# Two-layer mixture-of-experts kernel: reordering the last attention window, its chunks and its weight split

## The chip, the cores and the metric

One core of a Trainium2 chip runs the whole program. The metric is the device time of one execution in microseconds; the median of three runs of the kernel before is 1303.91 us (1302.14 to 1304.94).

## The reference, cut to what matters

`x` holds 2 sequences of 1024 tokens with 256 features. Six residual steps follow one another: half a mixture of experts (8 experts, top 2), an RWKV-like attention, half the same mixture; then for the second layer:

```python
x = x + 0.5 * _L1_ffn_ref(_layernorm(x), ...)    # 32 experts of width 96, top 6, and a shared expert of width 192
x = x + _L1_attn_ref(_layernorm(x), ...)
x = x + 0.5 * _L1_ffn_ref(_layernorm(x), ...)    # the same weights again
# _L1_attn_ref: Q, K, V = split(X @ W_in.T + b_in); Q, K = rope(Q), rope(K)
#   A = sum over tokens of (K / |K|) * V;  Y = A * Q;  return Y @ W_out.T + b_out + X
# _L1_ffn_ref: scores = sigmoid(x @ gate_w); top 6, weights normed to 1
#   routed = sum over the chosen experts of weight * (silu(x wg) * (x wu)) wd;  shared = silu(x sg) * (x su) @ sd
```

The attention needs a sum over all 1024 tokens of a sequence before any of its outputs.

## The kernel before, in words

The tokens lie in SBUF as `XT`, 16 tiles of 128 tokens; a block `b` is four tiles (512 tokens), and two blocks make a sequence. The four mixtures are f = 0 to 3. Each engine has its own instruction stream, written out by hand, and semaphores tie them; a stream is strictly in order, so an instruction that waits holds all that stand behind it on its engine.

A mixture f has two parts. In its preparation, for each block: the norm's statistics (`stats`, DVE, lines 1839 to 1849), root and reciprocal (`std`, ACT; `offsets`, DVE, 1854 and 1856), the normed rows `xnt` (`rows`, ACT, line 1360), their transposes (`turn`, PE, 757 to 762, eight transposes of 128x128, of which all wait for the fourth tile of rows), a copy and a high and low half (`plain`, `split_high` on ACT, 1749 and 1752; `split_low` on DVE, 2497), the gate logits (`logits_of`, PE), `score` (ACT), `chosen` (DVE, 1890 to 1931: the top 6 as a mask), `rank` (PE, sums over tokens), `slots` (DVE, 1933 to 2009: each token's place in the table of its expert, written by line 1986). Then POOL scatters the rows of `xnt` to DRAM (`scatter_tile`, line 638), one indirect DMA per tile and choice, 24 per block and 96 for f = 3. `slots(3, 3)` ends with eight short steps that find each pair's expert. The shared expert is worked off in chunks, two per block (`gate_up`, `down` on PE; `silu`, `hidden` on ACT; `prod`, `low_hidden`, `finish` on DVE, `finish` adding the sum to `XT` at line 2061).

In the second part, `tiles(f)`, SP loads pairs of 128 gathered tokens (line 545), PE turns them, computes gate and up (`up`, line 910) and down, and POOL gathers the results (line 653). For f = 3 the down weights are split in a high and a low part first: `down_high` (ACT, 1501, four copies), `down_back` (ACT, 1509, eight copies of the high part into PSUM), `down_low` (DVE, 2523, eight subtractions). The second `up` of `tiles(3)` and the first down wait for all eight.

Between `tiles(2)` and `tiles(3)` stands the window. It holds the attention and the whole preparation of mixture 3. For each block g PE makes eight sets in PSUM banks n % 4 (`attend`: k1, k2, v1, v2, ss, q1, q2, rn); DVE rotates k1 and q1 (`rotated`, 2454 to 2458), weights the values (`key_values`, `key_inverse`), and sums them against rn (`key_sums`, 2479). After both blocks of a sequence `weighted` makes `WSH` (2487), `project_out` multiplies it with the queries (PE, 1256) into banks 0 to 3, and `added` adds it to `XT` (2493), one call for two tiles. POOL adds the attention's own norm as a residual (`residual(b)`, 658 and 660, for blocks 2 and 3 in this window) once the rows of block b are there, and it stands ahead of the scatters in POOL's stream. The chunks of mixture 3 follow the routing, one at the logits of block 2 and the rest behind block 3's `chosen`, with the parts of the down split between them. SP waits for all scatters and for the last `finish` before it loads for `tiles(3)`.

Of the kernel before, what the change touches and what calls it, by code (L numbers as in the profile page):

```python
# [6 lines left out]
F32 = mybir.dt.float32  # L7
# [25 lines left out]
PARTS0 = 0  # L33
HALVED0 = 0
# [42 lines left out]
TAKEN = {"k1": 3, "v1": 4, "v2": 5, "q1": 8, "rn": 10}  # L77
# [14 lines left out]
def chunk_table():  # L92
# [35 lines left out]
def program(nc, x_in, w0s, w0e, wsq, wa0, w1, wsh1, win, wout, gate0, gate1, vecs, rope, bcol, brow, ident_in, tri_in, cvec_in, xd, yd, out):  # L128
# [21 lines left out]
    with ExitStack() as ctx:  # L150
# [127 lines left out]
        xh31_at = upto[0]  # L278
        XH[3, 1] = inside("XH3_1", [P, 2, KD, BT], F32R)
        assert upto[0] <= tb_end, (upto[0], tb_end)  # L280
# [12 lines left out]
        XH[3, 2] = inside("XH3_2", [P, 2, KD, BT], F32R)  # L293
        XH[3, 3] = inside("XH3_3", [P, 2, KD, BT], F32R)
        S3 = inside("S3", [P, 2, BT], F32)
        HL3 = inside("HL3", [P, 2, 2, BT], F32R)
        assert upto[0] <= xh31_at
# [13 lines left out]
        TX, TGU, THT, TY = 0, 1, 3, 7  # L311

# [193 lines left out]
        def _(sp):  # L506
# [86 lines left out]
            sp.wait_ge(CK.sum, GROUP["s", 3, 3] + 1)  # L593
# [160 lines left out]
        def _(pe):  # L754
            mm = nc.tensor.matmul

            def turn(norm, b, src, bank):
                pe.wait_ge(norm.rows, NT * (b + 1))
                for k in range(KD):
                    for a in range(NT):  # L760
                        last = nc.tensor.transpose(ps[:, bank + k, a * P:(a + 1) * P], src[:, b * NT + a, k * P:(k + 1) * P], ident[:, :])  # L761
                last.then_inc(norm.turned, 1)
# [101 lines left out]
            def tiles(f, beside=None, ahead=None, between=None):  # L864
# [16 lines left out]
                def hturned(q):  # L881
                    pe.wait_ge(TL.hid, q + 1)
                    pe.wait_ge(TL.hT, q)
                    if f == 3:
                        pe.wait_ge(TL.hlo, HALVED0 + q - q0)
# [7 lines left out]
                def up(q):  # L893
# [6 lines left out]
                    if f == 3 and i == 1:  # L900
                        pe.wait_ge(ew_lo, PARTS0 + 8)
# [12 lines left out]
                def down_rows(q):  # L914
# [3 lines left out]
                    if f == 3:  # L918
                        if q == q0:
                            pe.wait_ge(ew_lo, PARTS0 + 8)  # L920
                        pe.wait_ge(TL.hlo, HALVED0 + q - q0 + 1)
# [295 lines left out]
            def attend(s, n0, n1):  # L1217

                for n in range(n0, n1):
# [5 lines left out]
                    elif s:  # L1225
                        pe.wait_ge(A1.add, n + 1)
# [20 lines left out]
            def project_out(s):  # L1247
                pe.wait_ge(A1.wo, s + 1)
                pe.wait_ge(A1.qrot, 2 * s + 2)
                pe.wait_ge(A1.q2, 2 * s + 2)  # L1250
                for h in range(ST // 2):
                    for i in range(2):
                        a = ((2 * h + i) % NT) * P
                        dst = ps[:, h, i * D:(i + 1) * D]
# [31 lines left out]
            def window():  # L1286
                n = len(SETS)
                chunks = [ch for b in range(NB) for ch in RUN["s", 3, b][0]]
                attend(0, 0, 2 * n)
# [29 lines left out]
                gate_up(chunks[1], taken_over(chunks[1]))  # L1319
                down(chunks[0])  # L1320
                next_rank(3)
                for i in range(2, len(chunks)):
                    gate_up(chunks[i], taken_over(chunks[i]))
                    down(chunks[i - 1])
                    if i == 3:
# [23 lines left out]
        def _(act):  # L1349
# [147 lines left out]
            def down_high(g):  # L1497
                if g == 0:
                    act.wait_ge(CK.gu, RUN["s", 3, 0][0][-1].i + 1)
                    act.wait_ge(A1.add, 8)  # L1500
                fn(WDH[:, 8 * g:8 * g + 8, :], WDR[:, 8 * g:8 * g + 8, :], ACT.Copy).then_inc(ew_hi, 1)

            def down_back(g):
                act.wait_ge(ew_hi, g // 2 + 1)
                if g:
                    act.wait_ge(ew_lo, g)
# [251 lines left out]
            def window():  # L1758
# [30 lines left out]
                split_high(2)  # L1789
                score(3, 2, A_BANK + 1)  # L1790
                rows(F_NORM[3], 3, XT[:, tiles_of(3), :])
                plain(3)
                split_high(3)
                score(3, 3, A_BANK + 1)
                for i, ch in enumerate(chunks):
                    silu(ch)
                    hidden(ch)
                    if i % 2:
                        down_high(i // 2)
                    if i >= 3:  # L1800
                        down_back(i - 3)
                for g in (5, 6, 7):
                    down_back(g)
# [15 lines left out]
        def _(dve):  # L1819
# [654 lines left out]
            def key_sums(g):  # L2474
                A1.ready(dve, g, "rn")
                dve.wait_ge(A1.taken, TAKES * g + TAKEN["q1"])
# [4 lines left out]
                dve.wait_ge(A1.taken, TAKES * (g + 1))  # L2481
# [8 lines left out]
            def added(s, h):  # L2490
                rows = XT[:, s * ST + 2 * h:s * ST + 2 * h + 2, :].rearrange("p t d -> p (t d)")
                dve.wait_ge(A1.y, 4 * s + h + 1)
                tt(rows, rows, ps[:, h, :], ALU.add).then_inc(A1.add, 1)
# [23 lines left out]
            def down_low(g):  # L2517
                dve.wait_ge(ew_back, g + 1)
                if g == 0:
# [5 lines left out]
            def window(first):  # L2525
# [17 lines left out]
                key_inverse(0)  # L2543
                rotated(0, "q1", QT[:, 0, 0, :], A1.qrot)
                key_sums(0)
# [11 lines left out]
                added(0, 0)  # L2557
                added(0, 1)
                dve.wait_ge(A1.add, 2)
                stats(F_NORM[f], 0, XT[:, tiles_of(0), :])  # L2560
                added(0, 2)
                offsets(F_NORM[f], 0, True)
# [158 lines left out]
```

## Time and profile before

| what | value |
|---|---|
| median of three runs | 1303.91 us |
| profiled execution: span | 1495.7 us |
| PE busy, DVE, ACT, POOL | 1178.6, 743.8, 536.0, 596.8 us |
| mean granted PE clock | 0.865 |
| window between `tiles(2)` and `tiles(3)` | about 998 to 1262 us |

Times in a view of the trace are microseconds from the start of the span, durations in its groups nanoseconds. The profiled execution has no time of its own beside its span. PE and PEld are matmul and weight load, DVE VectorE, ACT ScalarE, POOL GpSimd, SP the queue that issues plain DMAs. `[x <- y]` behind an instruction is how long its engine stood idle before it and what ended that.

### The profile page before, as it was taken

How to read it: one execution, taken by the hardware profiler on the slowest of the kernel's cores; microseconds unless marked ns; L12 is line 12 of the kernel's file. 1: busy time of each engine (PE TensorE's matmuls, PEld its weight loads, DVE VectorE, ACT ScalarE, POOL GpSimd, SP SyncE). 2: the span in 40 equal slices, each digit the busy share in tenths (PEclk: the TensorE clock that was granted, in tenths of full speed). 3: DMA queues.
4: the chain of work that ended last, by engine and by line, in shares of the span. 5: the costliest groups of instructions: out<-in, count | busy, mean ns of one | idle time of the engine just before them, and what ended most of it. 6: DMA issues, size and time to landing. Idle time of an engine off the chain costs nothing.

```text
span 1495.7 us, 20198 instructions
## 1 busy us (share of the span) xinstructions
PE 1178.6 (79%) x6031; PEld 960.0 (64%) x6031; DVE 743.8 (50%) x2333; ACT 536.0 (36%) x1012; POOL 596.8 (40%) x579
## 2 busy tenths in 40 slices
PE   4799988979989898854768998897755436988884
PEld 4677755666778676633557987875434225978784
DVE  5553465564546536413445555678644214633443
ACT  2323344554533234321413433442303115644442
POOL 3661352211124213674550155662453730045554
PEclk9789999998989999865868999898875667998897
DMA  9523439400002573331426687760121212676676
GB/s 331 211 72 107 143 96 308 141 1 0 1 29 107 206 260 119 117 114 64 173 76 216 195 241 237 219 191 4 60 79 41 105 53 63 198 208 205 204 223 191
DMA packets 125302, 209.81 MB, mean 140 GB/s; under 512 B 15296, under 2 KB 104768, under 8 KB 123328
## 3 DMA queue, kind: packets, MB, share of 16 engines
q1 hardware_dynamic: 100624, 141.38, 28.7%
q0 software_dynamic: 24576, 67.14, 14.4%
q8 instruction: 56, 0.92, 0.3%
q14 instruction: 46, 0.38, 0.1%
HBM read 129.29 MB, written 101.19 MB: 154 GB/s over the span
## 4 chain that ended last, share of the span: by engine, by line
PE 48%; DVE 18%; issue 13%; another core or an unknown queue 10%; ACT 6%; POOL 3%; DMA 1%; SPq 0%; DVEq 0%; POOLq 0%; ACTq 0%
PE ps L910 15%; PE ps L932 6%; PE ps L877 5%; PE ps L817 4%; PE ps L829 4%; PE ps L889 3%; PE ps L1093 2%; PE ps L1100 2%; ACT xnt L1360 1%; PE ps L927 1%; PE ps L1244 1%; DVE HL L2047 1%; POOL xd L638 1%; PE ps L925 1%
## 5 line engine op out<-in xcount | busy, mean ns | idle before, releaser
L653 POOL DMA_INDIRECT G<-yd,slot_of x256 | 253.1, 989 | 424.6 <-issue 189.3
L638 POOL DMA_INDIRECT xd<-xnt,slot_of x256 | 251.4, 982 | 224.4 <-DVE slot_of L1986 136.9
L910 PE MATMUL ps<-WE,xT 128*128 x1016 | 200.7, 343 | 5.6 <-issue 3.9
L2102 DVE TENSOR_TENSOR hid<-hid,ps 128x192 f32<-128x192 f32 (+2 forms) x168 | 65.4, 389 | 247.9 <-ACT hid L1551 198.1
L910 PEld LDWEIGHTS ps<-WE,xT 128*128 128x128 f32 x1016 | 174.0, 202 | 9.9 <-issue 9.7
L1522 ACT ACTIVATE xT<-ps 128x512 f32<-128x512 f32 (+1 forms) x168 | 99.2, 590 | 156.9 <-PE ps L877 121.6
L877 PE MATMUL ps<-ident,xd_in 128*128 128x128 f32 x664 | 108.2, 287 | 44.2 <-ACT xT L1522 24.0
L2081 DVE SCALAR_TENSOR_TENSOR XT<-G,wt,XT 128x256 f32<-128x256 f32 x256 | 123.8, 494 | 27.5 <-DMA G<-yd,slot_of 17.0
L1551 ACT ACTIVATE hid<-ps 128x192 f32<-128x192 f32 (+2 forms) x168 | 60.4, 359 | 192.1 <-PE ps L910 139.9
L877 PEld LDWEIGHTS ps<-ident,xd_in 128*128 128x128 f32 x664 | 84.5, 148 | 60.6 <-issue 37.0
L1379 ACT ACTIVATE S<-ps 128x512 f32<-128x512 f32 (+1 forms) x72 | 42.6, 592 | 179.1 <-PE ps L817 140.1
L910 PE MATMUL ps<-W0E,xT 128*128 x312 | 103.3, 475 | 0.1
L2109 DVE COPY yo<-ps 128x512 f32<-128x512 f32 x104 | 70.9, 682 | 59.6 <-PE ps L932 30.7
L2047 DVE TENSOR_TENSOR HL<-S,HL 128x512 fp32r<-128x512 f32 (+1 forms) x72 | 51.9, 721 | 92.8 <-ACT HL L1388 87.0
L817 PE MATMUL ps<-XH,W0S 128*128 128x512 f32 x288 | 87.5, 456 | 8.9 <-issue 7.1
L932 PE MATMUL ps<-W0E,hT 88*128 x312 | 80.0, 401 | 13.3 <-issue 10.0
L889 PE MATMUL ps<-ident,hid 128*96 128x128 f32 (+1 forms) x410 | 75.5, 282 | 17.1 <-issue 7.6
L1388 ACT ACTIVATE HL<-S 128x512 fp32r<-128x512 f32 (+1 forms) x72 | 45.0, 625 | 104.8 <-DVE S L2042 70.7
L932 PEld LDWEIGHTS ps<-W0E,hT 88*128 88x128 f32 x312 | 61.6, 200 | 29.0 <-issue 15.1
L761 PE MATMUL ps<-ident,xnt 128*128 128x128 f32 x232 | 40.4, 332 | 50.3 <-ACT xnt L1360 41.3
L817 PEld LDWEIGHTS ps<-XH,W0S 128*128 128x128 f32 x288 | 62.7, 224 | 26.3 <-issue 12.0
L910 PEld LDWEIGHTS ps<-W0E,xT 128*128 128x128 f32 x312 | 58.7, 198 | 28.3 <-issue 5.1
(245 smaller groups left out, 2173.6 us busy)
## 6 DMA issues: line engine op xcount, KB each, us to landing
xd_in<-xd SPq DMA_DIRECT2D x164, 256.0 KB
yd<-yo SPq DMA_DIRECT2D x164, 256.0 KB
WE<-w SPq DMA_DIRECT2D x8, 1280.0 KB
W0E<-w0e SPq DMA_DIRECT2D x1, 4864.0 KB
xd<-xnt,slot_of POOLq DMA_INDIRECT x256
G<-yd,slot_of POOLq DMA_INDIRECT x256
W0E<-w0e SPq DMA_DIRECT2D x1, 3040.0 KB
XT<-x_in SPq DMA_DIRECT2D x4, 512.0 KB, 6.1
```

Of the source, the lines that this page charges most:

```text
L638: nc.gpsimd.indirect_dma_start(xd[f // 2][:, :], bass.IndirectOffsetOnAxis(ap=slot_of[:, t, k:k + 1], axis=0), xnt[:, t, :], None).then_in ...
L653: nc.gpsimd.indirect_dma_start(G[:, n % G_RING, :], None, yd[f // 2][0:min(ly.early[t][k] * 2, ly.TILES) * P, :], bass.IndirectOffsetOnAxi ...
L817: last = mm(ps[0:ch.H, ch.bank + u, :], l, r, start=(i == 0), stop=(i == len(terms) - 1))
L877: last = nc.tensor.transpose(ps[:, TX, (2 * a + k) * P:(2 * a + k + 1) * P], xd_in[:, q % X_RING, a, k * P:(k + 1) * P], ident[:, :])
L889: last = nc.tensor.transpose(ps[0:ly.part, hth, n * P:(n + 1) * P], hid[:, q % 2, a, c * ly.part:(c + 1) * ly.part], ident[:, :])
L910: last = mm(dst, xT[:, q % 2, a, k, :], flat[:, bass.ds(expert[2 * q + a] + k * 2 * ly.H, 2 * ly.H)], start=(k == 0), stop=(k == KD - 1))
L932: last = mm(ps[:, ty, a * D:(a + 1) * D], hT[0:ly.part, q % 2, a * ly.parts + c, :], flat[0:ly.part, bass.ds(expert[2 * q + a] + ly.down_a ...
L1522: fn(xT[:, q % 2, 0:m].rearrange("p a k t -> p (a k t)"), ps[:, TX, 0:m * D], ACT.Copy).then_inc(TL.xT, 1)
L2047: tt(hl[0:ch.H, 1, ch.i % 2, :], S_of[ch.kind][0:ch.H, ch.i % 2, :], hl[0:ch.H, 0, ch.i % 2, :].bitcast(F32), ALU.subtract).then_inc(CK.lo, 1)
L2081: stt(XT[:, t, :], G[:, n % G_RING, :], wt[:, t, k:k + 1], XT[:, t, :], ALU.mult, ALU.add).then_inc(g_used, 1)
L2102: tt(hid[:, q % 2, 0:m, 0:ly.H], hid[:, q % 2, 0:m, 0:ly.H], src, ALU.mult).then_inc(TL.hid, 1)
L2109: copy(yo[:, q % Y_RING, 0:m].rearrange("p a d -> p (a d)"), ps[:, down_bank(f, q), 0:m * D]).then_inc(TL.y, 1)
```

## The change

- `turn` waits for the rows tile by tile and transposes tile by tile; it is used in all four preparations and in both attentions.
- In the window `key_sums` comes before `rotated(g, "q1")` on DVE, and `rotated` of the second block behind `weighted`. Bank q1 is thus taken last and rn earlier.
- `project_out` waits for the queries of its half only and writes to banks 0, 4, 1, 2. `summed(b)` adds two tiles, takes their `bn_stats`, and again, for each half. Block 0's sums and `offsets` come before the statistics of the attention norm's block 3, whose root and rows move on ACT behind the rows of block 0 and `score(3, 0)`; POOL's `residual(3)` waits for them.
- Chunks 0, 1 and 2 stand between the routing steps of blocks 2 and 3 on PE, ACT and DVE. Chunks of blocks 0 and 1 use banks 2 and 3 alone. `down_high` stands behind chunks 4 to 7, `down_back` and `down_low` behind all chunks, in the order 2 to 7, 0, 1.
- SP waits for the last `gate_up` in place of the last `finish`. Some buffers move (`XH[3, 2]` to QT, `XH[3, 3]` to KB, `HL3` to the place of a staging buffer).

```diff
-            add(("s", f, b), ("s1", "s3")[f - 2], f, b, SH1, (2, 6))
+            add(("s", f, b), ("s1", "s3")[f - 2], f, b, SH1, (2, 6) if f == 2 or b >= 2 else (2, 2))
+        OUT_BANK = (0, A_BANK, 1, 2)
+        SPLIT_ORDER = (2, 3, 4, 5, 6, 7, 0, 1)
@@ sync
-            sp.wait_ge(CK.sum, GROUP["s", 3, 3] + 1)
+            sp.wait_ge(CK.gu, RUN["s", 3, 3][0][-1].i + 1)
@@ tensor
             def turn(norm, b, src, bank):
-                pe.wait_ge(norm.rows, NT * (b + 1))
-                for k in range(KD):
-                    for a in range(NT):
+                for a in range(NT):
+                    pe.wait_ge(norm.rows, NT * b + a + 1)
+                    for k in range(KD):
...
             def project_out(s):
                 pe.wait_ge(A1.wo, s + 1)
-                pe.wait_ge(A1.qrot, 2 * s + 2)
-                pe.wait_ge(A1.q2, 2 * s + 2)
                 for h in range(ST // 2):
+                    if h % 2 == 0:
+                        pe.wait_ge(A1.qrot, 2 * s + 1 + h // 2)
+                        pe.wait_ge(A1.q2, 2 * s + 1 + h // 2)
...
-                gate_up(chunks[0], taken_over(chunks[0]))
+                chunk(0)
                 logits_of(2)
                 next_turn(3)
                 next_rank(2)
+                chunk(1)
                 logits_of(3)
+                chunk(2)
+                next_rank(3)
                 pe.wait_ge(F_NORM[3].lo, NB)
...
-                for i in range(2, len(chunks)):
+                for k in range(3, len(chunks)):
@@ scalar
-                std(AT_NORM, 3)
-                rows(AT_NORM, 3, XT[:, tiles_of(3), :])
                 flipped(2, B_BANK)
                 std(F_NORM[3], 0)
                 rows(F_NORM[3], 0, XT[:, tiles_of(0), :])
+                std(AT_NORM, 3)
                 std(F_NORM[3], 1)
                 plain(0)
                 split_high(0)
                 score(3, 0, A_BANK + 1)
+                rows(AT_NORM, 3, XT[:, tiles_of(3), :])
                 rows(F_NORM[3], 1, XT[:, tiles_of(1), :])
...
+                for i in range(8):
+                    down_back(i)
@@ vector
+            def summed(b):
+                s = b // 2
+                for i in range(2):
+                    h = 2 * (b % 2) + i
+                    added(s, h)
+                    dve.wait_ge(A1.add, 4 * s + h + 1)
+                    for a in (2 * i, 2 * i + 1):
+                        last = nc.vector.bn_stats(st6[:, a, :], XT[:, b * NT + a, :])
...
-                rotated(1, "q1", QT[:, 1, 0, :], A1.qrot)
                 key_sums(1)
                 weighted()
+                rotated(1, "q1", QT[:, 1, 0, :], A1.qrot)
+                summed(0)
+                offsets(F_NORM[f], 0, True)
                 last_stats()
                 offsets(AT_NORM, 3, True)
...
+                summed(1)
                 offsets(F_NORM[f], 1, True)
...
                 chosen(f, 2)
+                prod(chunks[0])
+                low_hidden(chunks[0])
                 slots(f, 2, A_BANK)
                 split_low(3)
+                prod(chunks[1])
                 chosen(f, 3)
-                prod(chunks[0])
-                low_hidden(chunks[0])
+                low_hidden(chunks[1])
+                finish(chunks[1])
+                prod(chunks[2])
                 slots(f, 3, A_BANK)
+                low_hidden(chunks[2])
...
+                for i in range(8):
+                    down_low(i)
```

## Rows read from the trace of the kernel before

**Rows 1.** The profile's page: the span, and the chain of waits by engine.
```profile
span 1495.7 us, 20198 instructions
...
PE 48%; DVE 18%; issue 13%; another core or an unknown queue 10%; ACT 6%; POOL 3%; DMA 1%; SPq 0%; DVEq 0%; POOLq 0%; ACTq 0%
```
**Rows 2.** The chain of waits, 1061 to 1262 us: start, length, what.
```profile
1123.98 10.92 another core or an unknown queue
...
1185.53 32.93 another core or an unknown queue
```
**Rows 3.** Timeline of POOL: start us, us, engine, line, operation [idle before it <- releaser].
```profile
1061.77 1.01 POOL L638 DMA_INDIRECT xd<-xnt,slot_of  x1 [18.36 <-DVE slot_of L1986]
...
1101.22 0.96 POOL L638 DMA_INDIRECT xd<-xnt,slot_of  x1 [9.33 <-DVE slot_of L1986]
...
1153.94 0.96 POOL L638 DMA_INDIRECT xd<-xnt,slot_of  x1 [22.72 <-DVE slot_of L1986]
...
1213.44 0.96 POOL L638 DMA_INDIRECT xd<-xnt,slot_of  x1 [0.30 <-issue]
```
**Rows 4.** Timeline of DVE, third norm's routing: `chosen(3, 0)`, slots of blocks 0 and 3.
```profile
1052.03 0.20 DVE L1898 MAX8 t<-sc 128x8 f32<-128x40 f32 x1 [1.08 <-issue]
...
1061.31 0.18 DVE L1986 TENSOR_SCALAR slot_of<-v 128x32 int32<-128x32 f32 x1
...
1170.46 0.18 DVE L1986 TENSOR_SCALAR slot_of<-v 128x32 int32<-128x32 f32 x1
```
**Rows 5.** Timeline, end of the window and start of `tiles(3)`.
```profile
1218.49 1.22 DVE L2061 SCALAR_TENSOR_TENSOR XT<-ps,XT 128x1024 f32<-128x1024 f32 x1 [32.95 <-remote]
...
1251.48 1.23 DVE L2061 SCALAR_TENSOR_TENSOR XT<-ps,XT 128x1024 f32<-128x1024 f32 x1 [3.02 <-PE ps L829]
...
1252.73 9.11 SPq L545 DMA_DIRECT2D xd_in<-xd  x6
...
1257.36 1.22 DVE L2523 TENSOR_TENSOR WDF<-WE,ps 128x1024 fp32r<-128x1024 f32 x1 [1.15 <-ACT ps L1509]
...
1259.73 1.22 DVE L2523 TENSOR_TENSOR WDF<-WE,ps 128x1024 fp32r<-128x1024 f32 x1 [1.15 <-ACT ps L1509]
...
1261.58 2.65 PE L910 MATMUL ps<-WE,xT 128*128 x8
```
**Rows 6.** Timeline of DVE and PE, second half-sequence of batch element 0.
```profile
1028.64 0.75 DVE L2454 SCALAR_TENSOR_TENSOR TA<-ps,BCOL,COS 128x512 f32<-128x512 f32 x1 [0.96 <-PE ps L1244]
...
1030.15 1.05 PE L1237 MATMUL ps<-ident,RN 128*128 128x128 f32 x8
...
1033.25 0.62 DVE L2487 TENSOR_SCALAR WSH<-WOUT,apart 128x256 f32<-128x256 f32 x2
```
**Rows 7.** Timeline of DVE, ACT and POOL, 1035 to 1054 us.
```profile
1035.63 0.17 DVE L1849 TENSOR_SCALAR rs<-mv 128x4 f32<-128x4 f32 x1
...
1036.48 2.07 ACT L1360 ACTIVATE xnt<-XT,rs 128x256 f32<-128x256 f32 x4 [0.44 <-DVE rs L1856]
...
1038.63 2.35 POOL L658 TENSOR_TENSOR XT<-XT,xnt 128x1024 f32<-128x1024 f32 x1 [16.11 <-ACT xnt L1360]
...
1040.26 0.75 DVE L1849 TENSOR_SCALAR rs<-mv 128x4 f32<-128x4 f32 x1
...
1041.06 2.35 POOL L660 TENSOR_TENSOR XT<-XT,BROW 128x1024 f32<-128x1024 f32 x1
...
1041.72 1.71 DVE L1856 SCALAR_TENSOR_TENSOR rs<-mv,rs 128x4 f32<-128x4 f32 x1
...
1051.89 2.06 ACT L1360 ACTIVATE xnt<-XT,rs 128x256 f32<-128x256 f32 x4
```
**Rows 8.** Timeline of PE: a turn of a block, cold, warm; and what line 761 waits for.
```profile
14.95 1.94 PE L761 MATMUL ps<-ident,xnt 128*128 128x128 f32 x8 [14.95 <-ACT xnt L1360]
...
1031.04 1.04 PE L761 MATMUL ps<-ident,xnt 128*128 128x128 f32 x8
...
  ACT xnt L1360: 46.3, 13
```

More of the change, by code:

```diff
@@ L32 @@
 X2_RING = 3
-PARTS0 = 0
-HALVED0 = 0
 class Layer:
@@ L292, in program @@
         WDH = inside("WDH", [P, E1, D], F32R)
[L293 to L297, printed above, removed]
+        wdh_end = upto[0]
+        XH[3, 2] = sb("XH3_2", [P, 2, KD, BT], F32R, qt_at)
+        kb_at = qt_at + 4 * 2 * KD * BT
+        XH[3, 3] = sb("XH3_3", [P, 2, KD, BT], F32R, kb_at)
+        S3 = sb("S3", [P, 2, BT], F32, wdh_end)
+        assert wdh_end + 4 * 2 * BT <= qt_at
+        hl3_at = xt_at
+        HL3 = sb("HL3", [P, 2, 2, BT], F32R, hl3_at)
+        assert kb_at + 4 * 2 * KD * BT <= hl3_at and hl3_at + 4 * 4 * BT <= xh31_at
         WDF = sb("WDF", [P, E1, LY[1].EW], F32R, w_at)
@@ L1288, in window, with chunk @@
                 chunks = [ch for b in range(NB) for ch in RUN["s", 3, b][0]]
+                def chunk(k):
+                    gate_up(chunks[k], taken_over(chunks[k]))
+                    if k:
+                        down(chunks[k - 1])
                 attend(0, 0, 2 * n)
@@ L1316, in window @@
                 next_rank(2)
+                chunk(1)
                 logits_of(3)
+                chunk(2)
+                next_rank(3)
                 pe.wait_ge(F_NORM[3].lo, NB)
-                gate_up(chunks[1], taken_over(chunks[1]))
-                down(chunks[0])
-                next_rank(3)
-                for i in range(2, len(chunks)):
-                    gate_up(chunks[i], taken_over(chunks[i]))
-                    down(chunks[i - 1])
-                    if i == 3:
+                for k in range(3, len(chunks)):
+                    chunk(k)
+                    if k == 5:
                         expert_row(3, A_BANK)
@@ L1789, in window @@
                 split_high(2)
+                silu(chunks[0])
                 score(3, 2, A_BANK + 1)
                 rows(F_NORM[3], 3, XT[:, tiles_of(3), :])
+                hidden(chunks[0])
                 plain(3)
                 split_high(3)
+                silu(chunks[1])
                 score(3, 3, A_BANK + 1)
[L1795 to L1803, printed above, removed]
+                hidden(chunks[1])
+                for k in range(2, len(chunks)):
+                    silu(chunks[k])
+                    hidden(chunks[k])
+                    if k >= 4:
+                        down_high(SPLIT_ORDER[2 * (k - 4)] // 2)
+                for i in range(8):
+                    down_back(i)
             act.wait_ge(consts_ready, 1)
@@ L2475, in key_sums @@
                 A1.ready(dve, g, "rn")
-                dve.wait_ge(A1.taken, TAKES * g + TAKEN["q1"])
+                dve.wait_ge(A1.taken, TAKES * g + TAKEN["v2"])
                 bank = (len(SETS) * (g % 2) + SETS.index("rn")) % 4
@@ L2480, in key_sums @@
                         accum_out=apart[:, k, g % 2:g % 2 + 1]).then_inc(A1.taken, 1)
-                dve.wait_ge(A1.taken, TAKES * (g + 1))
+                dve.wait_ge(A1.taken, TAKES * g + TAKEN["rn"])
             def weighted():
@@ L2492, in added @@
                 dve.wait_ge(A1.y, 4 * s + h + 1)
-                tt(rows, rows, ps[:, h, :], ALU.add).then_inc(A1.add, 1)
+                tt(rows, rows, ps[:, OUT_BANK[h], :], ALU.add).then_inc(A1.add, 1)
+            def summed(b):
[6 more added lines that the diff above has]
+                        last = nc.vector.bn_stats(st6[:, a, :], XT[:, b * NT + a, :])
+                st.do(last)
+                st.sync()
+                for a in range(NT):
+                    last = nc.vector.bn_aggr(mv[:, b * NT + a, :], st6[:, a, :])
+                st.do(last)
+                st.sync()
+                ts(rs[:, 0, tiles_of(b)], mv[:, tiles_of(b), 1], EPS, None, ALU.add).then_inc(F_NORM[3].var, 1)
             def split_low(b):
@@ L2596, in window @@
                 chosen(f, 2)
+                prod(chunks[0])
+                low_hidden(chunks[0])
                 slots(f, 2, A_BANK)
                 split_low(3)
+                prod(chunks[1])
                 chosen(f, 3)
-                prod(chunks[0])
-                low_hidden(chunks[0])
+                low_hidden(chunks[1])
+                finish(chunks[1])
+                prod(chunks[2])
                 slots(f, 3, A_BANK)
-                for i in range(1, len(chunks)):
+                low_hidden(chunks[2])
+                for i in range(3, len(chunks)):
                     prod(chunks[i])
                     low_hidden(chunks[i])
-                    if i == 3:
+                    if i == 5:
                         experts(f, A_BANK)
```

66 lines of the change are left out of this document (24 added, 42 removed).

## The prediction

> **What bounds the kernel now.** I read the page first. The span is 1495.7 us against a median run of 1303.91, so the profiled execution is 191.8 us longer than a run; its chain of waits gives 48% to PE, 18% to DVE, but also 13% to "issue" and 10% to "another core or an unknown queue" [rows 1]. The reader is to see that some of this chain cannot be in the runs. The change works in the window between `tiles(2)` and `tiles(3)`, 998 to 1262 us, so I read the chain there next. Its two longest pieces are 32.93 and 10.92 us in which DVE stood before an instruction whose inputs were long there [rows 2]. All such gaps lie in stretches in which POOL issues scatters. I take them, as an estimate, for a cost of the profiled execution: the whole chain has 311 us of pieces over 1.3 us of those two kinds (56 pieces, counted by me), more than the 191.8 to be explained, so most but not all of them must be absent in the runs. I argue with the gaps taken out, and keep the opposite as a rival.
>
> Third view, POOL. It issues its 96 scatters of the third norm from 1061.77 on; it idled 9.33 us before block 1 and 22.72 before block 2, waiting for `slots`; from 1153.94 it ran 48 in a row, the last at 1213.44: 59.5 us over 47 steps, 1.266 us each [rows 3]. On DVE's side the gaps of the chain between 1061.8 and 1153.9 sum to about 35 us, more than POOL's two idle times together (32.1). Without them `slots(3, 2)` would be ready at 1119 (subtraction) to 1123.5 (my reckoning instruction by instruction, PE at its lower clock), and POOL is through blocks 0 and 1 at 1061.77 + 48 x 1.266 = 1122.5. So in the runs POOL is all but never starved: **from the first slots on, the window lasts as long as 96 scatters, 121.5 us**, to 1183.3 on this axis.
>
> Fourth view, the tail. `finish` of chunk 1 starts at 1218.49 and that of chunk 7 at 1251.48, 33.0 us for six chunks with parts of the down split between them; then SP loads at 1252.73, the last down part starts at 1259.73, the first `up` at 1261.58 [rows 5]. The tail's head is `slots(3, 3)` at 1170.46 [rows 4]. Without gaps, 8 us lead from there to `finish(1)` (estimate: eight short steps, three 0.7 us operations and a down), then 33.0 + 1.2 + 8.3. That is 50.5 us behind `slots(3, 3)`, which stands 17 us behind `slots(3, 2)`: 1119 to 1123.5 becomes 1186.5 to 1191. The scatters end at 1183.3, must land, be loaded, turned and copied before the first `up`: 1190 to 1193. The two paths lie within a few us of each other, POOL's the later.
>
> **Part by part.**
> *Key sums before the query rotation.* Now DVE rotates q1 from 1028.64 while PE makes q2 and rn; rn's matmuls start at 1030.15; WSH starts at 1033.25 [rows 6]. The new order waits for rn (end 1031.2, pushed about 1.2 us by k2 of the second set, which now waits for q1 to be taken later), so `weighted` comes about 0.7 us later, and the 3.1 us of rotation now lie behind it, where PE projects out h 0 anyway. Cost on the chain: 0.7 us.
>
> *Added by halves, three banks moved, third norm of block 0 first.* The sums and statistics are the same instructions: four additions, four `bn_stats` pairs, aggregates. From WSH to `chosen(3, 0)` I count 18.3 us in the new order; before it is 1052.03 - 1033.87 = 18.2 [rows 4, 6]. What is gained by not waiting for the block's second projection is spent on the rotation and on `last_stats`. `chosen(3, 0)` starts about 0.9 us later than now.
>
> *Row step of block 3 of the attention norm and its residual moved.* ACT's four activations (2.07 us [rows 7]) now stand between `score(3, 0)` and the rows of block 1, on whose turn PE's `next_rank(0)` is queued. Worked through: rows of block 1 end at 1055.9 instead of 1051.89 + 2.06 = 1053.95 [rows 7], turn per tile at 1056.6, rank at 1057.5. This makes `slots(3, 0)` 1.5 us later, at 1063. POOL's `residual(3)` moves with the rows: its two 2.35 us additions run now from 1038.63 to 1043.41 [rows 7], and would run from 1053.9 to 1058.7, right inside `chosen(3, 0)`. What that costs, the rows show: the 4-element DVE scalar operation that takes 0.17 us takes 0.75 and ends when POOL's first addition ends, and the next one takes 1.71 and ends with the second [rows 7]. The statistics and the additions out of PSUM beside them take their usual time. In the new place the mask and the first prefix sum of `chosen` have two SBUF inputs or the scalar form: each waits out one addition, 1.3 and 2.3 us. So `slots(3, 0)` comes at 1066.1, **4.8 us later than now**. The bounds are 1.5 (nothing is held) and 6.2 (both additions held in full).
>
> The Trainium skill (SBUF — State Buffer, Who interferes with whom) says that a DVE instruction with two SBUF inputs and a GpSimd instruction that reads SBUF exclude each other for the whole of the one that came first, and that a scalar operation in its two-port mode does too. By that rule the trace agrees, and it speaks against this part of the change: 4.8 us and not 1.5.
>
> *From there.* POOL needs no further idle time: by the same reckoning `slots(3, 2)` comes 60.1 us behind `slots(3, 0)`, and 48 scatters take 60.8. POOL ends 4.8 us later; if it was starved by up to 1 us before, the difference is 4. I take **+4**.
>
> *Chunks between routing steps.* Chunks 0 to 2 are done before or beside `slots(3, 3)`, which grows later by some 4 to 8 us but is needed by POOL only 13 us after that. Behind it stay five chunks at 33.0 / 6 = 5.5 us, 27.5 us, and 2 us of column sums.
>
> *Down split behind them.* Now half of it is hidden between chunks; then the eight pairs run one behind the other, 1259.73 - 1257.36 = 2.37 us each [rows 5], 19 us. Sum behind `slots(3, 3)`: 48.5 us against 50.5. With `slots(3, 3)` 4 to 8 us later the split ends 2 to 6 us later than now, about where the later POOL path has its first `up`. Taken at nothing more, covered by the scatters; if that cover is gone it costs up to 3 us.
>
> *SP waits for the last gate and up instead of the last sum.* Some 6 us earlier, but behind 96 scatters that land later still: nothing.
>
> *Turns tile by tile.* `turn` is called in every stage, 29 times. PE stood waiting for ACT's rows of line 1360 in 13 of the records [rows 8], and for the lead rows in three more; nine such turns lie outside this window. A turn takes 1.94 us with PE just out of idle and 1.04 warm [rows 8]; six of its eight transposes now run under ACT's rows. That saves 0.8 us in six of the nine and 1.45 in three, 9.2 us if all are on the path. At the lower end, nothing, where DVE, POOL or a DMA is late next. Nearly all nine stand in the profiled chain, but in the first stage and in mixing PE's next wait is often for DVE. I take two thirds, **-6**.
>
> Sum: +4 - 6 = -2. On the profiled execution 1493.7 us, on the median 1302.
>
> **The rivals.**
> Turns pay in full and POOL's additions hold nothing: -9.2 + 1.5, **1296**. For it: the chain; against it: the held 0.75 and 1.71 us.
> Slower: the late first slots decide. `slots(3, 0)` is 4.8 us or more late, every scatter behind it with it, and the saved transposes outside are absorbed by the next wait (-1): **1308**. It wins as soon as the window loses more than the turns give. For it: POOL without idle time; against it: turns on the chain.
> The gaps belong to the kernel too: then the scatters end before the chunks, and the tail is what counts: now 1261.58 - 1218.49 = 43 us; after, five chunks without splits between and the split, 41 to 46, or 8 less if a further chunk gets through: **1292 to 1307**. Against it: 191.8 us that have to be somewhere.
> It does nothing: banks and chunks are reordered under the scatters and the turns are hidden: **1304**.
>
> **How the numbers follow.** About 0.2%, 2.6 us, can be told from no change. Forecast 0.30 (1298 to 1306; mostly a little faster or same), full turns 0.25, slower 0.25, own gaps 0.10, nothing 0.10. Faster: 0.13 + 0.25 + 0.05; same: 0.14 + 0.03 + 0.10; slower: 0.03 + 0.25 + 0.02. The range runs from the first rival with the bound of its turns (1293) to the slower one with its 6.2 us and split uncovered (1311).
>
> **What would show it.** Right: POOL's additions of block 3 beside a DVE operation of the routing that takes over 1 us; first scatter 3 to 6 us further behind the start of the window; eight down parts 2.37 us apart behind the last chunk; turns that end within 0.6 us of the rows. Wrong: POOL starved between the blocks although DVE has no gaps, a first `up` waiting for the last down part long after the last scatter, or a window shorter by more than the gaps differ.

## The result and the profile after

The kernel after takes 1305.6 us (median of nine runs, 1301.71 to 1308.1), the kernel before 1302.14 beside it (nine runs). The ratio is 1.0036 with a 95% interval of 1.0021 to 1.0051: **slower by 4.7 us (2.7 to 6.6)**. The two medians alone lie 3.5 us apart (1.0027), inside the same interval; the text goes by the ratio. The forecast was 1302 and leaned to faster; the time lies inside its range, but the direction was wrong. Of the rivals, "slower: the late first slots decide" (1308) came true in kind: the first slots are late and the turns give nothing, with 3.3 us in place of 4.8.

The page of the kernel after: span, and the chain of waits by engine and by line. They answer to [rows 1]. Line numbers of the kernel after are 4 to 29 higher than those of before.
```profile
span 1299.9 us, 20205 instructions
...
PE 56%; POOL 15%; DVE 11%; issue 9%; ACT 4%; DMA 4%; SPq 1%; POOLq 0%; ACTq 0%; DVEq 0%
PE ps L914 18%; POOL xd L642 13%; PE ps L936 8%; PE ps L881 5%; PE ps L821 4%; PE ps L833 4%; PE ps L893 3%; PE ps L1097 3%; DMA xd<-xnt,slot_of 2%; PE ps L1104 2%; PE ps L1248 2%; ACT xnt L1370 1%; POOL G L657 1%; PE ps L929 1%; PE ps L930 1%
```
No piece of this chain is "another core or an unknown queue", and the 191.8 us by which the first profile of before was longer than a run are gone. So I compare with a second profile of the kernel before, the first experiment. In the experiments, times are also given from the start of the window, the first k1 matmul of its attention: 916.50 us on the axis of after, 918.10 on that of the second profile of before.

POOL of after: the residual of block 3, the first and the last scatter, as in [rows 3, 7].
```profile
968.28 2.36 POOL L662 TENSOR_TENSOR XT<-XT,xnt 128x1024 f32<-128x1024 f32 x1 [26.82 <-ACT xnt L1370]
970.72 2.34 POOL L664 TENSOR_TENSOR XT<-XT,BROW 128x1024 f32<-128x1024 f32 x1
...
980.51 1.01 POOL L642 DMA_INDIRECT xd<-xnt,slot_of  x1 [7.45 <-DVE slot_of L1998]
...
1102.43 0.96 POOL L642 DMA_INDIRECT xd<-xnt,slot_of  x1 [0.30 <-issue]
```
The 96 scatters stand back to back: 121.92 us for 95 steps. POOL is never starved, as worked out, but there is less to spare: `slots(3, 2)` is ready 2.5 us before POOL starts its 49th scatter, where the second profile of before has 4.8.

DVE of after, `chosen(3, 0)` and the slots of block 0, as in [rows 4].
```profile
969.00 1.73 DVE L1933 TENSOR_SCALAR mask<-rest 128x128 fp32r<-128x128 f32 x1
970.76 2.35 DVE L1935 TENSOR_TENSOR prefix<-prefix,mask 128x32 fp32r<-128x32 f32 x1
...
974.83 0.29 DVE L1963 TENSOR_SCALAR base<-ps 128x128 f32<-128x128 f32 x1 [0.84 <-PE ps L790]
...
980.05 0.18 DVE L1998 TENSOR_SCALAR slot_of<-v 128x32 int32<-128x32 f32 x1
```
The mask started during POOL's first addition and ended with it (970.73 against 970.64), the first prefix sum took as long as the second (2.35 against 2.34).

The end of the window in after, as in [rows 5]: last scatter parts, load, turn, first `up`.
```profile
1100.92 1.22 DVE L2552 TENSOR_TENSOR WDF<-WE,ps 128x1024 fp32r<-128x1024 f32 x1 [1.15 <-ACT ps L1519]
...
1103.29 1.22 DVE L2552 TENSOR_TENSOR WDF<-WE,ps 128x1024 fp32r<-128x1024 f32 x1 [1.15 <-ACT ps L1519]
...
1104.92 12.31 SPq L549 DMA_DIRECT2D xd_in<-xd  x8
...
1107.75 1.09 PE L881 MATMUL ps<-ident,xd_in 128*128 128x128 f32 x4 [22.25 <-DMA xd_in<-xd]
...
1110.83 2.92 PE L914 MATMUL ps<-WE,xT 128*128 x8
```
PE stood still for 22.25 us until the first gathered tokens were there; the last down part, 2.37 us behind its neighbour, was ahead of them by 3 us. The load starts 2.49 us behind the last scatter and the first `up` 8.40 behind it.

### The profile page after: what moved, and what is told of

The parts are those of the page before. It is cut to its first block, busy times and chain, and to the rows that moved or that the text cites. A ratio compares the mean times of both kernels' runs of the same rounds, so it can differ in the third digit from the quotient of the medians.

```text
span 1299.9 us, 20205 instructions
## 1 busy us (share of the span) xinstructions
PE 1110.8 (85%) x6031; PEld 911.0 (70%) x6031; DVE 744.1 (57%) x2333; ACT 539.3 (41%) x1015; POOL 596.6 (46%) x579
## 4 chain that ended last, share of the span: by engine, by line
PE 56%; POOL 15%; DVE 11%; issue 9%; ACT 4%; DMA 4%; SPq 1%; POOLq 0%; ACTq 0%; DVEq 0%
PE ps L914 18%; POOL xd L642 13%; PE ps L936 8%; PE ps L881 5%; PE ps L821 4%; PE ps L833 4%; PE ps L893 3%; PE ps L1097 3%; DMA xd<-xnt,slot_of 2%; PE ps L1104 2%; PE ps L1248 2%; ACT xnt L1370 1%; POOL G L657 1%; PE ps L929 1%; PE ps L930 1%
## 5 line engine op out<-in xcount | busy, mean ns | idle before, releaser
L914 PE MATMUL ps<-WE,xT 128*128 x1016 | 189.9, 330 | 0.2
L914 PEld LDWEIGHTS ps<-WE,xT 128*128 128x128 f32 x1016 | 164.9, 193 | 1.5 <-issue 1.1
L881 PE MATMUL ps<-ident,xd_in 128*128 128x128 f32 x664 | 103.4, 278 | 53.7 <-DMA xd_in<-xd 48.1
L936 PE MATMUL ps<-W0E,hT 88*128 x312 | 76.9, 389 | 6.2 <-DVE yo L2121 6.2
L821 PE MATMUL ps<-XH,W0S 128*128 128x512 f32 x288 | 76.9, 419 | 1.5 <-POOL W0S L610 1.2
L619 POOL TENSOR_TENSOR rs<-rs,small 128x4 f32<-128x4 f32 x17 | 17.7, 1044 | 119.2 <-DVE rs L1861 119.0
L821 PEld LDWEIGHTS ps<-XH,W0S 128*128 128x128 f32 x288 | 56.6, 202 | 14.3 <-POOL W0S L610 1.6
L936 PE MATMUL ps<-WE,hT 96*128 x254 | 65.4, 379 | 0.0
```

The costliest lines, as they stand in the source:

```text
L821: last = mm(ps[0:ch.H, ch.bank + u, :], l, r, start=(i == 0), stop=(i == len(terms) - 1))
L881: last = nc.tensor.transpose(ps[:, TX, (2 * a + k) * P:(2 * a + k + 1) * P], xd_in[:, q % X_RING, a, k * P:(k + 1) * P], ident[:, :])
L914: last = mm(dst, xT[:, q % 2, a, k, :], flat[:, bass.ds(expert[2 * q + a] + k * 2 * ly.H, 2 * ly.H)], start=(k == 0), stop=(k == KD - 1))
L936: last = mm(ps[:, ty, a * D:(a + 1) * D], hT[0:ly.part, q % 2, a * ly.parts + c, :], flat[0:ly.part, bass.ds(expert[2 * q + a] + ly.down_a ...
```

## The experiments

Eleven experiments follow. The first is one execution of the kernel before; the others are twelve executions each, in five rounds beside the kernel before. In the table, times are in us from the start of the window in the one profile of each kernel. "Weighted, 1st" is the first `WSH`, and "last down part" the start of the last `down_low`. "Hold" is what POOL's residual of block 3 added to DVE operations ahead of the first slots. The first `up` follows 8.3 to 8.6 us behind the last scatter in all.

| kernel | ratio to before (95%) | weighted, 1st | slots(3, 0) | last scatter | first up | last down part | hold |
|---|---|---|---|---|---|---|---|
| before_again | 1 | 32.01 | 60.24 | 182.27 | 190.76 | 179.39 | 2.1 |
| turn_only | 0.9989 (0.9972 to 1.0006) | 32.00 | 59.51 | 182.09 | 190.40 | 179.21 | 2.1 |
| after | 1.0036 (1.0021 to 1.0051) | 32.11 | 63.55 | 185.93 | 194.33 | 186.79 | 3.7 |
| after_old_turn | 1.0033 (1.0017 to 1.0050) | 32.09 | 63.85 | 185.11 | 193.69 | 187.12 | 3.4 |
| small_residual | 0.9992 (0.9974 to 1.0010) | 32.10 | 60.81 | 183.69 | 192.15 | 187.25 | 0 |
| before_placed | 0.9992 (0.9975 to 1.0009) | 32.01 | 59.94 | 181.32 | 189.88 | 179.73 | 0.3 |
| before_placed_turn | 0.9996 (0.9975 to 1.0016) | 32.02 | 57.03 | 179.27 | 187.91 | 176.36 | 0.3 |
| placed_turn_again | 0.9994 (0.9979 to 1.0008) | 32.02 | 59.87 | 182.62 | 191.21 | 182.48 | 0.3 |
| after_placed | 1.0011 (0.9995 to 1.0027) | 33.66 | 61.67 | 183.74 | 192.25 | 184.26 | 0.3 |
| after_placed_keys | 1.0016 (1.0001 to 1.0031) | 32.02 | 61.16 | 184.16 | 192.72 | 183.19 | 0.3 |
| old_sp_wait | 1.0024 (1.0005 to 1.0043) | 32.10 | 64.05 | 186.78 | 195.33 | 190.41 | 4.0 |
| norm3_first | 1.0020 (1.0005 to 1.0035) | 33.65 | 64.33 | 186.54 | 195.11 | 187.07 | 2.8 |

**before_again**: the kernel before, unchanged, profiled once more.

> The kernel before, unchanged, for a second profile. Theory A (the profiled gaps of before were the profiler's): a span near 1300 us, no piece of 10 us or more charged to an unknown queue between first and last scatter of the third norm, POOL scattering 96 times nearly without idle time, 121 to 123 us. Rival (the gaps belong to the kernel): a span over 1400 us with DVE standing 10 us and more beside the scatters again. From the profile of after, whose window from the first k1 matmul to the first up of tiles(3) is 194.2 us: if the window is where the 4.7 us went, this one has 189 to 191 us; if it is outside, 193 to 195.

It took 1299.91 us with a span of 1298.1 us. Its POOL and, around the residual, its DVE:
```profile
955.49 2.35 POOL L658 TENSOR_TENSOR XT<-XT,xnt 128x1024 f32<-128x1024 f32 x1 [15.04 <-ACT xnt L1360]
957.92 2.35 POOL L660 TENSOR_TENSOR XT<-XT,BROW 128x1024 f32<-128x1024 f32 x1
...
978.80 1.01 POOL L638 DMA_INDIRECT xd<-xnt,slot_of  x1 [18.53 <-DVE slot_of L1986]
...
1100.37 0.96 POOL L638 DMA_INDIRECT xd<-xnt,slot_of  x1 [0.30 <-issue]
```
```profile
957.12 0.75 DVE L1849 TENSOR_SCALAR rs<-mv 128x4 f32<-128x4 f32 x1
...
958.58 1.71 DVE L1856 SCALAR_TENSOR_TENSOR rs<-mv,rs 128x4 f32<-128x4 f32 x1
...
970.99 0.19 DVE L1921 TENSOR_SCALAR mask<-rest 128x128 fp32r<-128x128 f32 x1
971.22 0.19 DVE L1923 TENSOR_TENSOR prefix<-prefix,mask 128x32 fp32r<-128x32 f32 x1
...
973.13 0.29 DVE L1951 TENSOR_SCALAR base<-ps 128x128 f32<-128x128 f32 x1 [0.85 <-PE ps L786]
```
And its end of the window:
```profile
1097.49 1.22 DVE L2523 TENSOR_TENSOR WDF<-WE,ps 128x1024 fp32r<-128x1024 f32 x1 [1.15 <-ACT ps L1509]
...
1102.86 10.17 SPq L545 DMA_DIRECT2D xd_in<-xd  x7
...
1105.79 1.09 PE L877 MATMUL ps<-ident,xd_in 128*128 128x128 f32 x4 [16.59 <-DMA xd_in<-xd]
...
1108.86 2.93 PE L910 MATMUL ps<-WE,xT 128*128 x8
```
The gaps of 10.92 and 32.93 us [rows 2] and POOL's idle times of 9.33 and 22.72 us [rows 3] belonged to that one profiled execution. The kernel before, too, issues its 96 scatters without a pause. The two held operations are there again to 0.01 us [rows 7]; the mask and the prefix sum are free in before and held in after. Window to window, the first slots come 3.3 us later in after and the first `up` 3.6: the window of before lasts 190.76 us, inside the 189 to 191 written down for a loss in the window. What follows `up` lasts 189.2 us before and 189.1 after.

**turn_only** is before with the turns tile by tile, **after_old_turn** is after without them:
```diff
-                pe.wait_ge(norm.rows, NT * (b + 1))
-                for k in range(KD):
-                    for a in range(NT):
+                for a in range(NT):
+                    pe.wait_ge(norm.rows, NT * b + a + 1)
+                    for k in range(KD):
```

> The kernel before with the turns tile by tile and nothing else. Theory A (my prediction): six of eight transposes go under ACT's rows in nine turns outside the window and some inside: 3 to 9 us faster than before, ratio 0.993 to 0.998. Rival B (the turns are what made it slower, by where PE now waits or by its clock): 2 to 5 us slower, 1.002 to 1.004. Rival C (hidden): within 0.15%.

> The changed kernel with the turns waiting for all four tiles again. Theory A: the turns gave 3 to 9 us, so this is slower than after by as much, 1.006 to 1.010 against before. Rival B (turns cost): 0.998 to 1.001 against before. Rival C (turns do nothing, the window costs it all): 1.0036 as the change itself, 1.002 to 1.005.

The two ratios, 0.9989 and 1.0033 against 1.0036, leave at most a few us for the turns and most likely about one or none. The 3 to 9 us of the expectation did not come; its rival "hidden" did. The two sides of the turn's line tell why. In before_again, what ended PE's idle time ahead of the turns (us, times), and who waited for them:
```profile
  ACT xnt L1360: 36.4, 13
...
who waited for it (us, times):
  ACT G L1749: 3.2, 4
  ACT XP L1406: 1.9, 1
  ACT X L1445: 0.5, 2
```
and the same in turn_only:
```profile
  ACT xnt L1360: 27.1, 29
...
who waited for it (us, times):
  ACT XP L1406: 1.1, 1
  ACT G L1749: 0.8, 1
```
PE waited less for rows, but only 5.6 us of waiting had hung on the end of a turn at all, 1.9 of which are left. Four of the seven waits are the copies of `plain` in this very window (L1749), where the scatters set the end; outside of it the only one above 0.5 us is the copy of XP, 1.9 us, which became 1.1. The first turn of the kernel shows the cover. before_again:
```profile
14.80 1.94 PE L761 MATMUL ps<-ident,xnt 128*128 128x128 f32 x8 [14.80 <-ACT xnt L1360]
...
15.09 2.08 ACT L1360 ACTIVATE xnt<-XT,rs 128x256 f32<-128x256 f32 x4 [0.43 <-DVE rs L1856]
...
17.08 1.00 ACT L1406 ACTIVATE XP<-ps 128x1024 f32<-128x1024 f32 x1
18.13 3.58 PE L981 MATMUL ps<-graw,XP 128*128 128x8 f32 x16 [1.38 <-ACT XP L1406]
```
and turn_only:
```profile
13.90 2.07 PE L761 MATMUL ps<-ident,xnt 128*128 128x128 f32 x8 [13.90 <-ACT xnt L1360]
...
15.66 2.07 ACT L1360 ACTIVATE xnt<-XT,rs 128x256 f32<-128x256 f32 x4 [0.43 <-DVE rs L1856]
...
17.64 1.00 ACT L1406 ACTIVATE XP<-ps 128x1024 f32<-128x1024 f32 x1
18.69 3.58 PE L981 MATMUL ps<-graw,XP 128*128 128x8 f32 x16 [2.72 <-ACT XP L1406]
```
ACT makes the next block's rows (2.07 us) before it copies this block's turn (1.94 us), so the turn had been hidden all along. Here it ends 1.3 us earlier measured from those rows, and PE's next wait grows from 1.38 to 2.72 us by the same 1.3.

**small_residual** is after with the two additions of POOL's `residual(3)` on 4 of 256 columns; it leaves out most of block 3's residual and bias.
```diff
+                w = 4 if b == 3 else D
-                nc.gpsimd.tensor_tensor(XT[:, tiles_of(b), :], XT[:, tiles_of(b), :], xnt[:, tiles_of(b), :], ...
+                nc.gpsimd.tensor_tensor(XT[:, tiles_of(b), 0:w], XT[:, tiles_of(b), 0:w], xnt[:, tiles_of(b), 0:w], ...
```

> The changed kernel, with POOL's two residual additions of block 3 cut to 4 of 256 columns (so most of block 3's normed residual and output bias is left out). In the profile of after DVE's mask takes 1.73 us instead of 0.23 and the first prefix sum 2.35 instead of 0.19, each ending with one of POOL's additions. Theory A (they delay the first slots, and all scatters behind them): mask and prefix sum at 0.2 us, the first scatter about 3 us earlier behind the window's start, 2.5 to 3.7 us faster than after, ratio against before 1.000 to 1.0015. Rival (something else is late next, or the scatters are not the bound): unchanged at 1.0036, plus or minus 0.001.

```profile
969.64 0.22 POOL L663 TENSOR_TENSOR XT<-XT,xnt 128x16 f32<-128x16 f32 x1 [26.84 <-ACT xnt L1371]
...
970.35 0.19 DVE L1934 TENSOR_SCALAR mask<-rest 128x128 fp32r<-128x128 f32 x1
970.57 0.19 DVE L1936 TENSOR_TENSOR prefix<-prefix,mask 128x32 fp32r<-128x32 f32 x1
```
With POOL's two additions short, both DVE operations are back at 0.19 us, the first slots come 2.7 us earlier than in after, the first `up` 2.2, and the ratio falls by 0.0044. That is 5.7 us, more than the window shows and more than was expected (1.000 to 1.0015); the two intervals together allow 2.7 to 8.7, so the excess isn't resolved.

Why 2.7 and not the full 3.7 of the hold? PE and the next step of DVE:
```profile
970.66 1.91 PE L766 MATMUL ps<-ident,xnt 128*128 128x128 f32 x8
...
973.46 0.29 DVE L1964 TENSOR_SCALAR base<-ps 128x128 f32<-128x128 f32 x1 [1.81 <-PE ps L791]
```
The sums of `next_rank(0)` now stand behind block 1's turn on PE, and DVE waits 1.81 us for them in place of 0.84. In after the same turn (1.91 us from 969.30) was over before the held prefix sum was. Two delays that run side by side don't add: the shorter one shows only when the longer is gone.

**before_placed** keeps the additions of before whole and moves them to a place where they hold next to nothing of DVE: one wait on POOL. **before_placed_turn** has the turns tile by tile besides; **placed_turn_again** is the same kernel once more.
```diff
+                if b == 3:
+                    pool.wait_ge(F_NORM[3].scale, 2)
```

> The kernel before; POOL's residual of block 3 waits for the offsets of the third norm's block 1, so its two additions run beside the k1 rotation and not beside the statistics. In the second profile of before those hold DVE for 0.58 and 1.55 us ahead of the first slots. Theory A (POOL's additions decide when the 96 scatters start, and these decide the window): the first scatter comes 1.5 to 2.1 us earlier, at 58.6 to 59.2 behind the first k1 matmul against 60.7; the first up as much earlier; ratio 0.9984 to 0.9990. Rival (the held time is not on the path): first scatter at 60.5 to 60.9, ratio 0.9995 to 1.0005.

> The same with the turns tile by tile. Theory A: what the turns gave alone (first scatter 0.7 us earlier, 0.11% in all) adds up: first scatter at 57.9 to 58.5, ratio 0.997 to 0.999. Rival (turns are covered everywhere): the same as with the wait alone.

> The same kernel as before_placed_turn, once more: the kernel before with POOL's residual(3) held until block 1's root is there, and turns tile by tile. Only a repetition, to see what belongs to the edit and what to the single run. If its first slots at 57.0 us (60.2 before) belong to the edit, they are there again within 1 us, and if the window's 3 us are worth their time the ratio is 0.998 or less. Rival: they came from PE's clock in that one profile; then the first slots stand at 59 to 60 us and the ratio is 0.999 to 1.000.

The holds are gone but for 0.3 us, yet the first slots came at 59.94, 57.03 and 59.87 us, and no ratio is distinguishable from 1. Neither the 1.5 to 2.1 us expected of before_placed nor a ratio of 0.9990 or less showed. What differs between the three is PE's `project_out`, in before_placed:
```profile
951.29 10.09 PE L1258 MATMUL ps<-WSH,QT 128*128 128x256 f32 x32 [3.90 <-DVE WSH L2489]
...
957.97 0.69 DVE L2495 TENSOR_TENSOR XT<-XT,ps 128x512 f32<-128x512 f32 x1 [2.17 <-PE ps L1258]
```
and in before_placed_turn:
```profile
944.60 7.17 PE L1258 MATMUL ps<-WSH,QT 128*128 128x256 f32 x32 [2.33 <-DVE WSH L2489]
```
The same 32 matmuls took 10.09, 7.17 and (placed_turn_again) 10.01 us, and where they took 10 DVE waited 2.1 to 2.2 us for them. The granted clock during them was 0.71 (before_placed) and 0.72 (placed_turn_again) against 1.00 in before_placed_turn. It was 1.00 in before_again too, so the 3.2 us by which before_placed_turn has its first slots earlier are a comparison at the same clock: 1.8 of them are hold, 0.7 came from the turns in turn_only as well, and the rest is open. In the other two profiles the wait for PE uses nearly all of it up. One kernel, profiled twice, came out either way, so a single profile of such an edit proves little, and the twelve executions show no gain.

**after_placed** does the same for after (POOL's wait, and the rows of the attention norm's block 3 ahead of the third norm's second root on ACT); **after_placed_keys** also puts the rotation of q1 back ahead of the key sums.
```diff
+                if b == 3:
+                    pool.wait_ge(F_NORM[3].scale, 2)
+                rows(AT_NORM, 3, XT[:, tiles_of(3), :])
                 std(F_NORM[3], 1)
...
-                rows(AT_NORM, 3, XT[:, tiles_of(3), :])
```

> The changed kernel with the attention norm's rows of block 3 in front of the root of block 1 on ACT, where ACT stood idle, and the same wait in front of POOL's residual of block 3. Theory A: mask and first prefix sum back to 0.2 us, 3.7 us less ahead of the first slots: first scatter at 60.0 to 61.3 against 64.0, ratio 0.999 to 1.001 against before. The third slots then limit POOL: an idle time of 0.5 to 1.5 us before block 2, as with the small residual. Rival (the reordered sums cost, not POOL): 1.003 to 1.004.

> The same with the q1 rotation ahead of the key sums again, as in before. In the profile of after the second WSH comes 95.75 us behind the first k1 matmul against 89.27 before, 6.5 us later while the first slots are 3.3 later; DVE idles 3.5 us for rn ahead of the second key sums. Theory A (waiting for rn with the rotation behind it costs 2 to 3 us): the second WSH at 89 to 91, third slots 2 to 3 us earlier than with the placed residual alone, no idle time of POOL before block 2, ratio 0.9985 to 1.000. Rival (the order of the two is neutral): as with the placed residual alone.

Without leaving anything out, the move brings the ratio from 1.0036 to 1.0011, 3.3 us (0.4 to 6.1 by the two intervals), and the window from 194.33 to 192.25 although the first `WSH` came 1.5 us later in that profile (DVE waited 2.01 us for rn on PE). Both ratios lie just above the 0.999 to 1.001 and 0.9985 to 1.000 expected, and POOL did not stand idle before block 2. The key order shows no effect on the time (1.0011 and 1.0016): the second sequence's `WSH` lies at 92.75 us in after_placed and at 90.60 with the old order (95.75 in after), but the scatters of block 0 are on their way by then, and they set the end. The reason for the late one is DVE's wait for rn, in after:
```profile
1010.71 0.69 DVE L2491 SCALAR_TENSOR_TENSOR TA<-KB,ps 128x512 f32<-128x512 f32 x1 [3.47 <-PE ps L1241]
```

**old_sp_wait** puts SP's wait for the last `finish` back into after.
```diff
-            sp.wait_ge(CK.gu, RUN["s", 3, 3][0][-1].i + 1)
+            sp.wait_ge(CK.sum, GROUP["s", 3, 3] + 1)
```

> The changed kernel with one wait put back: SP waits for the last finish again, not for the last gate and up. My theory: the scatters land after both, so nothing moves; the first load stays some 2.5 us behind the last scatter, the first up some 8.5 us behind it, and the ratio to the kernel before stays at 1.0036 within 0.0015. Rival: the last finish of the changed kernel comes late enough to decide; then the first load follows finish of chunk 7, the first up comes 1 us or more later than the 8.5 us behind the last scatter, and the ratio rises to 1.0045 or more.

```profile
1106.10 0.96 POOL L642 DMA_INDIRECT xd<-xnt,slot_of  x1 [0.31 <-issue]
```
```profile
1108.59 6.30 SPq L549 DMA_DIRECT2D xd_in<-xd  x6
```
The load stands 2.49 us behind the last scatter, in after as well, and the first `up` 8.55 (8.40 in after). This wait shows no cost and no gain. The later end of its window comes from elsewhere: the second `WSH` lies at 98.13 us, 2.4 later than in after, and POOL stood 0.77 us before its 49th scatter, as in small_residual.

**norm3_first** puts the statistics, root and rows of the attention norm's block 3 back ahead of block 0's sums.
```diff
+                std(AT_NORM, 3)
+                rows(AT_NORM, 3, XT[:, tiles_of(3), :])
                 flipped(2, B_BANK)
...
-                summed(0)
-                offsets(F_NORM[f], 0, True)
                 last_stats()
                 offsets(AT_NORM, 3, True)
+                summed(0)
+                offsets(F_NORM[f], 0, True)
```

> The changed kernel with the attention norm's block 3 (statistics, root, rows) put back ahead of block 0's sums on DVE and ACT, and so POOL's residual(3) earlier too; chunks, split, banks and key order stay as in the change. Theory: its gain (no additions of POOL inside chosen(3, 0), 3.7 us) is used up by statistics and root standing ahead of block 0's own, some 3 us, so slots(3, 0) stands 62 to 64 us behind the window's start (60.2 before, 63.55 in the change) and the ratio lies at 1.001 to 1.004. Rival: the moved norm is the whole loss; then slots(3, 0) stands at 60 to 61 us and the ratio is 1.000 or less.

```profile
959.35 1.23 DVE L2521 TENSOR_SCALAR rs<-mv 128x4 f32<-128x4 f32 x1
...
961.07 1.93 DVE L1868 SCALAR_TENSOR_TENSOR rs<-mv,rs 128x4 f32<-128x4 f32 x1
```
The residual's additions (958.20 and 960.63) hold two other operations now, the third norm's own root of block 0, by 2.8 us in place of 3.7. The first slots came at 64.33 us, 1.5 of it from a late `WSH`. The old order is no better inside the changed kernel as far as the runs can tell: 1.0020 against 1.0036, with intervals that overlap. It removes one hold and brings another, so it does not separate the order from the hold.

## Why the prediction was wrong

**Failed step: "Turns tile by tile ... I take two thirds, -6".** It measured about 0 in after (1.0036 with, 1.0033 without: 0.4 us slower, -2.5 to +3.3) and -1.4 us in before (-3.6 to +0.8). The step counted turns that PE had waited to begin (13 waits of 46.3 us [rows 8]) and took each as a turn whose end someone awaits. The other half of the same view says who does: in the first profile of before it names four waits of 6.0 us in all, in the second seven of 5.6, and four of those seven (3.2 us) lie inside the window. Outside, 2.4 us could be had, and the one longer wait there shrank from 1.88 to 1.15 us. The chain of waits, on which nearly all nine turns stood, was no proof: where ACT's rows of 2.07 us run beside a turn of 1.94, a chain may lead through either. With -1 in place of -6 the sum would have been +3, inside the 2.7 to 6.6 measured.

**The window, +4: right in size**, +3.6 in the profiles (first `up`) and +3.3 at the first slots, against +4.8 reckoned; in part by luck, since its terms missed both ways:
- Hold in `chosen(3, 0)`: predicted 1.3 and 2.3, of which the sum used 3.3; measured (1.73 - 0.19) + (2.35 - 0.19) = 3.7. small_residual removes it and takes 2.7 us off the first slots, after_placed moves it and gains 0.0025 of the time. The Trainium skill (SBUF — State Buffer, Who interferes with whom) has the rule of mutual exclusion; by that rule the trace agrees, in after, in norm3_first and in before. But before had a hold of 2.1 us of its own in the same stretch, and the change took it away: only 1.6 of the 3.3 us are additional hold.
- `weighted` 0.7 later: measured 0.1. `chosen(3, 0)` 0.9 later: measured 0.4 earlier (50.58 against 50.98 us). That is no gain of the new order. Before has its 2.1 us of hold ahead of `chosen(3, 0)`, the change has it behind. Where both kernels hold 0.3 us and `project_out` takes 7.17 us in both (before_placed_turn and after_placed), the first slots stand 25.0 and 28.0 us behind `WSH`. So the reordered sums seem to cost some 3 us by themselves, from one profile of each kernel; after against before_again leaves 1.7 (3.3 less 1.6), and the two ratios (0.9996 and 1.0011) do not resolve it. The prediction had this at 0.1 us (18.3 against 18.2) because its 18.2 contained the hold.
- `next_rank(0)` queued behind block 1's turn, 1.5 us: there, but hidden by the hold. DVE waits 0.84 us for it in after and 0.85 in before, and 1.81 in small_residual, 1.0 more. The prediction added this term to the hold; the two overlap.
- POOL adds next to nothing: right, 121.9 and 121.6 us for the scatters.

**Chunks, split and SP, 0: right.** This term held because the scatters cover the tail, and not for the reason of its own sum. The split ends 49.7 us behind `slots(3, 3)` (48.5 predicted); in before it is 48.5 and not 50.5, so the new tail is 1.2 us longer and not 2 shorter. The last part now starts 7.5 us ahead of the first `up` instead of 11.4, still covered; old_sp_wait shows no price of the SP wait.

**The gaps: right** as an estimate for the first profile only. Added up again from the chain, the pieces over 1.3 us come to 271 us in 54, not 311 in 56, and those between 1061.8 and 1153.9 to 32 us, not 35; the argument needed more than 191.8 and about 32, and stands, if barely in the second. With the gaps taken out the window is bound by POOL in both kernels, and the rival that kept them falls.

**The rest.** The two profiles differ by only 1.8 us of span because after's began its window 1.6 us earlier; even one kernel, profiled twice, began it at 911.91 and at 918.16 us (before_placed_turn and placed_turn_again). The runs, not that pair of spans, carry the 4.7 us. Of the 4.7, 3.6 are seen in the window; the rest is within the interval. How the late 3.3 us divide between hold and order is shown only in part, as said above. No version was found that beats the kernel before: turn_only stands at 0.9989, the ones with the residual placed at 0.9992, 0.9996 and 0.9994, and all their intervals contain 1.

## What to carry to other kernels

A view of an instruction has two sides: the idle time before it says what it waits for, and only "who waited for it" says whether an earlier end is worth anything; multiply a saving by the second. When a step moves on one engine, look at what the work that follows it on other engines now runs beside: two additions of 2.35 us on POOL cost 3.7 us on DVE operations of 0.19, and putting them elsewhere (one wait, and ACT's rows moved) gave back 3.3 us (0.4 to 6.1) of a 4.7 us loss. Count what the old place cost too: here it was 2.1 us, and a price taken from a measured stretch may contain it. When one queue runs without a pause (96 scatters, 121.6 us), only the time of its first item and its length count, and reordering behind it is free and worthless as long as the later items are ready in time; with the second `WSH` at 98.13 us instead of 95.75, POOL stood 0.77 us.

## What the runs showed of the hardware that was not expected

- One profiled execution of a kernel was 191.8 us longer than a run, with DVE standing for up to 32.93 us before ready instructions while POOL issued scatters [rows 1, 2]; all other profiles, of the same kernel too, had none, with spans of 1288.3 to 1309.4 us. A second profile of the same kernel settled it.
- The same 32 matmuls of `project_out`, in the first sequence, took 7.17 us after PE had idled 1.4 to 2.3 us and 10.0 to 10.1 after 3.90 us; the granted clock was 1.00 and 0.71 to 0.72, the mean of a stretch at the two levels of 2.4 and 1.2 GHz. The idle time alone does not decide: in after_placed_keys they took 8.86 us at 0.81 after 2.35 us. One kernel showed both ends in two profiles (before_placed_turn and placed_turn_again). Edits of 2 us on DVE ahead of it can be undone by it.
- POOL can be held too: where a DVE operation had started first, POOL's second addition took 2.69 to 2.70 us in place of 2.35 (before_placed, after_placed), and of DVE's operations beside the two additions only two grew, from 0.69 to 0.80 us and from 0.17 to 0.32.
